# First pair's loads held until the last x tile has landed; the second FFN's rows normalised on ScalarE, its residual sum written in two halves

## The reference

```
x = x + 0.5 * ffn(layernorm(x))     # router to 8 experts, top 2, capacity 1537, softmax of the two logits
x = x + attention(layernorm(x))     # 16 heads of 16, rotary q and k, softmax, projection Wo and bias bo
x = x + 0.5 * ffn(layernorm(x))     # the same weights as the first
```

## Time and profile before

| what | value |
|---|---|
| median of three runs | 6290.88 us |
| the profiled execution | 6298.43 us, span 6296.6 us |
| TensorE busy | 6199.1 us (98%) |
| VectorE busy | 5929.1 us (94%) |
| ScalarE busy | 4830.8 us (77%) |
| POOL busy | 398.3 us (6%) |
| granted TensorE clock, mean | 0.988 |

### The profile page before, as it was taken

One profiled execution on the slowest core, in us unless ns is written; L12 is line 12 of the kernel. 1 busy time (PEld: TensorE's weight loads), 2 busy tenths in 40 slices (PEclk: granted clock), 3 DMA queues, 4 the chain that ended last, 5 costly groups with the idle time before them and its releaser, 6 DMA issues. The chain is left out here.

```text
span 6296.6 us, 158218 instructions
## 1 busy us (share of the span) xinstructions
PE 6199.1 (98%) x54276; PEld 2765.3 (44%) x54276; DVE 5929.1 (94%) x6835; ACT 4830.8 (77%) x8889; POOL 398.3 (6%) x604
## 2 busy tenths in 40 slices
PE   8998999999999999999999999999999999999999
PEld 6886333333333333333333333333333333334777
DVE  7998999999999999999999999999999999992877
ACT  4443488888888888888888888888888888886111
POOL 3443100000000000000000000000000000000221
PEclk9998699999999999999999999999999999999999
DMA  2334110101010101010101010101010101000110
GB/s 85 121 126 124 25 17 14 17 14 17 13 17 14 17 14 17 14 17 14 17 14 17 14 17 14 17 14 17 14 17 14 17 14 17 3 22 26 60 52 28
DMA packets 121411, 175.90 MB, mean 28 GB/s; under 512 B 62016, under 2 KB 78944, under 8 KB 117728
## 3 DMA queue, kind: packets, MB, share of 16 engines
q1 hardware_dynamic: 120928, 168.25, 11.8%
HBM read 98.47 MB, written 69.73 MB: 27 GB/s over the span
## 5 line engine op out<-in xcount | busy, mean ns | idle before, releaser
L1136 DVE TENSOR_REDUCE at_mx<-at_m 128x1 f32<-128x1024 f32 x4027 | 4927.9, 1224 | 47.6 <-PE at_m L1012 28.1
L1111 ACT ACTIVATE at_ex<-at_s 128x512 f32<-128x512 f32 x8192 | 4450.2, 595 | 612.9 <-PE at_s L1033 44.7
L1033 PE MATMUL at_s<-at_q,at_k 50*128 50x512 f32 x8192 | 2998.4, 444 | 0.0
L1012 PE MATMUL at_m<-at_k,at_q 48*128 48x512 f32 x8032 | 2927.1, 444 | 0.0
L1043 PE MATMUL at_po<-at_ex,at_v 128*32 128x256 f32 x32816 | 2625.8, 392 | 0.0
L1012 PEld LDWEIGHTS at_m<-at_k,at_q 48*128 48x128 f32 x8032 | 1184.3, 185 | 1658.7 <-DVE at_mx L1136 1590.5
L1043 PEld LDWEIGHTS at_po<-at_ex,at_v 128*32 128x32 f32 x32816 | 646.6, 108 | 1489.4 <-issue 749.9
L1033 PEld LDWEIGHTS at_s<-at_q,at_k 50*128 50x128 f32 x8192 | 1212.4, 185 | 42.6 <-ACT at_ex L1111 42.2
L987 POOL COPY at_v<-at_vst 128x1024 f32<-128x1024 f32 x16 | 16.7, 1041 | 4463.6 <-DMA at_vst<-v_by_head 4463.4
L1417 PE MATMUL bk_ps<-sh_weh,bk_xl 128*128 128x512 f32 x512 | 170.1, 413 | 20.2 <-DVE bk_acc L1547 20.1
L1459 ACT ACTIVATE bk_root<-bk_var 128x4 f32<-128x4 f32 x16 | 3.3, 205 | 218.0 <-DVE bk_var L1517 218.0
(11 more groups left out here) (194 smaller groups left out, 2989.9 us busy)
## 6 DMA issues: line engine op xcount, KB each, us to landing
at_q<-q_parts SPq DMA_DIRECT2D x96, 256.0 KB, 5.0
at_k<-k_parts SPq DMA_DIRECT2D x96, 256.0 KB, 6.3
q_parts<-fr_parts SPq DMA_DIRECT2D x64, 256.0 KB, 2.2
k_parts<-fr_parts SPq DMA_DIRECT2D x64, 256.0 KB, 2.4
attended<-at_o SPq DMA_DIRECT2D x256, 34.0 KB
fr_x<-in_x SPq DMA_DIRECT2D x16, 512.0 KB, 4.3
after_ffn<-fr_acc SPq DMA_DIRECT2D x16, 512.0 KB, 3.0
v_by_head<-fr_v SPq DMA_DIRECT2D x16, 512.0 KB, 4.4
```

The source lines that it names most:

```text
L1012: ins = pe.matmul(pm[w][:, h * QB:(h + 1) * QB], Q[p][rows, base + i * P:base + (i + 1) * P], K[p][rows, c * CW + h * QB:c * CW + (h + 1) ...
L1033: pe.matmul(ps[event(t) % NS], K[p][rows, j * P:(j + 1) * P], Q[p][rows, sb_ * QU + g * QB:sb_ * QU + (g + 1) * QB], start=True, stop=True ...
L1111: ac.activation(Ex[QUAD * (j % NX) + 2 * g + 1 - half][:, :], ps[event(t) % NS], ACT.Exp)\
L1136: ve.tensor_reduce(out=mx[u][:, i, c:c + 1], in_=first[(RED + k) % len(first)][:, 0:CW] if opens else pm[w][:, :], op=ALU.max, axis=AX.X)\
```

## The change

SP's wait: before the first pair's loads, SP waits until all x tiles of odd groups, the last of them tile 15, have landed. In the back phase, VectorE's `normal` becomes `newton`: the same five steps, and a sixth that forms nb = -mean * rs. ScalarE gets `normalise(g+1)`, four activations xn = src * rs + nb with per-row scale and bias, between the root and `turned`. The residual sum is cut in two calls: half 0 (tiles 0 and 1, from py[0]) follows the picks, half 1 stays at the body's end. Each half signals s_y, so all counts on s_y double, `spread_out` waits for half 0 of the previous group alone, and `project` gets a wait for both halves.

```diff
                     if isinstance(g, int) and g == NG - 2:
                         hold(sp, opening.s_one, 2, s_tick)
+                        hold(sp, s_x[(NG - 1) % 2], NG // 2 * DMA, s_tick)
                         for w in range(2):
...
                     pe.wait_ge(s_rec[u], it * DMA + DMA)
-                    need(pe, s_y, n)
+                    need(pe, s_y, n * 2 - 1)
                     pe.matmul(py[0][:, :], spread[:, :], rec[u][:, :], start=True, stop=True).then_inc(s_pr, 1)
...
                 def project(n):
                     need(pe, s_an, n + 1)
+                    need(pe, s_y, n * 2)
...
+                def normalise(n, src):
+
+                    need(ac, s_nw, (n + 1) * NEWTON)
+                    need(ac, s_tr, n)
+                    for i in range(TG):
+                        last = ac.activation(xn[:, i, :], src[:, i, :], ACT.Identity, bias=nb[:, i:i + 1], scale=rs[:, i:i + 1])
+                    last.then_inc(s_xn, 1)
...
                     if runs(g, 1):
                         take_root(g + 1)
+                        normalise(g + 1, y[1 - u])
                         turned(g + 1, 1 - u)
                         exponential(g + 1)
...
-                def add_residual(n, u):
-                    ve.wait_ge(s_py, n + 1)
-                    ve.wait_ge(s_xb, n + 1)
-                    for k in range(2):
-                        last = ve.tensor_tensor(y[u][:, 2 * k:2 * k + 2, :].rearrange("p i d -> p (i d)"), py[k][:, :],
-                                                xb[:, 2 * k:2 * k + 2, :].rearrange("p i d -> p (i d)"), ALU.add)
-                    last.then_inc(s_y, 1)
+                def add_residual(n, u, k):
+                    if k == 0:
+                        ve.wait_ge(s_py, n + 1)
+                        ve.wait_ge(s_xb, n + 1)
+                    ve.tensor_tensor(y[u][:, 2 * k:2 * k + 2, :].rearrange("p i d -> p (i d)"), py[k][:, :],
+                                     xb[:, 2 * k:2 * k + 2, :].rearrange("p i d -> p (i d)"), ALU.add).then_inc(s_y, 1)
...
-                def normal(n, src):
+                def newton(n):
 
                     ve.wait_ge(s_root, n + 1)
-                    ch = Chain(ve, s_nw, 5, n)
+                    need(ve, s_xn, n)
+                    ch = Chain(ve, s_nw, NEWTON, n)
...
+                    ch.add(ve.scalar_tensor_tensor(out=nb[:, :], in0=mv[:, :, 0], scalar=-1.0, in1=rs[:, :],
+                                                   op0=ALU.mult, op1=ALU.mult))
                     ch.close()
-                    need(ve, s_tr, n)
-                    for i in range(TG):
-                        last = ve.tensor_scalar(xn[:, i, :], src[:, i, :], mv[:, i, 0:1], rs[:, i:i + 1],
-                                                ALU.subtract, ALU.mult)
-                    last.then_inc(s_xn, 1)
...
                     if runs(g, 1):
                         pick(g + 1)
+                    if runs(g, 2):
+                        add_residual(g + 2, u, 0)
                     if isinstance(g, int) and g == 0:
                         invert_sums(ve, ahead, 1)
                     combine(g, u, it, 2, E // 2, E)
...
                     if runs(g, 2):
-                        add_residual(g + 2, u)
+                        add_residual(g + 2, u, 1)
```

More of the change, by code:

```diff
@@ L1258, in back_phase @@
     ROUTE = 7
+    NEWTON = 6
     with ExitStack() as ctx:
@@ L1278, in back_phase @@
         stats, mv = sb("stats", [P, TG, 6]), sb("mv", [P, TG, 2])
-        var, root, r0, r1, rs = (sb(n, [P, TG]) for n in ("var", "root", "r0", "r1", "rs"))
+        var, root, r0, r1, rs, nb = (sb(n, [P, TG]) for n in ("var", "root", "r0", "r1", "rs", "nb"))
         acc, acb = [sb(f"acc{u}", [P, TG, D]) for u in range(2)], sb("acb", [P, 2, D])
@@ L1476, in _ @@
                 take_root(0)
+                normalise(0, y[0])
                 turned(0, 0)
@@ L1496, in normalise_heads @@
                     last.then_inc(s_an, 1)
-                def add_residual(n, u):
-                    ve.wait_ge(s_py, n + 1)
-                    ve.wait_ge(s_xb, n + 1)
-                    for k in range(2):
-                        last = ve.tensor_tensor(y[u][:, 2 * k:2 * k + 2, :].rearrange("p i d -> p (i d)"), py[k][:, :],
-                                                xb[:, 2 * k:2 * k + 2, :].rearrange("p i d -> p (i d)"), ALU.add)
-                    last.then_inc(s_y, 1)
+                def add_residual(n, u, k):
[4 more added lines that the diff above has]
+                                     xb[:, 2 * k:2 * k + 2, :].rearrange("p i d -> p (i d)"), ALU.add).then_inc(s_y, 1)
                 def statistics(n, src):
-                    hold(ve, s_y, n + 1, s_tick)
+                    hold(ve, s_y, n * 2 + 2, s_tick)
                     for i in range(TG):
@@ L1592, in _ @@
                 normalise_heads(0, 0, 0)
-                add_residual(0, 0)
+                for k in range(2):
+                    add_residual(0, 0, k)
                 statistics(0, y[0])
-                normal(0, y[0])
+                newton(0)
                 normalise_heads(1, 1, 0)
@@ L1599, in _ @@
                 room(0)
-                add_residual(1, 1)
+                for k in range(2):
+                    add_residual(1, 1, k)
                 def body(g, u, it):
@@ L1607, in body @@
                     if runs(g, 1):
-                        normal(g + 1, y[1 - u])
+                        newton(g + 1)
                     combine(g, u, it, 1, 0, E // 2)
@@ L1634, in biased @@
                     if not (isinstance(n, int) and n == 0):
-                        hold(gp, s_y, n, s_tick)
+                        hold(gp, s_y, n * 2, s_tick)
                     for i in range(TG):
```

## The result

The changed kernel takes 6268.8 us (median of six runs, 6264.2 to 6273.7) beside 6291.6 of the kernel before (six runs, 6289.6 to 6301.9): 22.8 us less, a ratio of 0.9962 with a 95% interval of 0.9952 to 0.9972. Forecast were 6261.6 us, 29.3 less. Its profiled execution took 6268.08 us, span 6266.2, against 6298.43 and 6296.6 before; 30.4 us between the spans is more than between the medians, and the last experiments show which part of it is not the change.

The account below looks back on a forecast made before the run. TensorE, busy 98% of the span, was taken as the bound, so only its idle time could be won. Front 10.7 plus back 18.6 us gave 29.3 less, 6261.6 us; range 6251 to 6277 (own range 6256 to 6267).

Parts of the forecast that it names:

- the stall's size: Front, VectorE after its four statistics: the 12.22 us stall shrinks to 2.73, winning 9.4 us (bounds zero and 12.1).
- the clock: Front, TensorE after its gap: the clock stays at 2.4 GHz once the long gap goes, winning 1.3 us.
- group 0: Back phase, first group: of waits of 0.76 and 0.50 us, 0.5 is won; the inversion stays.
- 0.1 us for each turn: Back phase, TensorE's transposes: ScalarE's rows come level with need; 0.1 us a group charged, 15 x 0.1 = 1.5 us.
- The cover on SP: Front's end: later loads, issued near 518 and landed near 538, cost zero, hidden by 12 us on SP.
- The rule of the Trainium skill: Front: DMA engines serve rings in turn, so a backlog elsewhere holds no lone block; the front's gain would be zero.
- A group's 1.42 us: Back phase, TensorE's wait before the second tile's fourth chunk: 1.42 us won in each of twelve groups, 17.0 in all.
- Groups 13 and 14: Back phase, late groups: TensorE's waits give 2.0 us and 1.6 us; in the first of them the fetch stays.
- (a): Back phase: the turn takes over part of the wait; back 12.5, total 23.2 us, 6267.7; chance 0.14.
- (b): The front gives nothing: no fetch behind loads, or loads still catch a block; total 18.6 us, 6272.3; chance 0.18.
- (c): Back phase: ScalarE needs a 1.28 us table load before each group's rows; total 8.6 us, 6282; chance 0.04.
- (d): Start of attention: TensorE's clock stays half for longer; at 75 us more, 6299, slower than before; chance 0.04.

Follow-up runs that it names:

- the last experiments: The kernel before and the changed kernel each run once more, unchanged, for second traces: 6291.5 us and 6266.3 us.
- run 11: The kernel before once more, unchanged, for a second trace: 6291.5 us.
- run 12: The changed kernel once more, unchanged, for a second trace: 6266.3 us.
- run 4: The kernel before with only the residual sum cut in two halves, VectorE still normalising the rows: 6288.7 us, ratio 0.9992.
- run 7: The changed kernel with the second inversion of the sums in body 1 of the back phase instead of body 0: 6262.9 us.
- run 9: The changed kernel with the second inversion of the sums in the back phase's prologue instead of body 0: 6260.5 us, ratio 0.9948 to the kernel before.
- run 1: The kernel before with only SP's wait for the last x tile ahead of the first loads of attention: 6284.1 us, ratio 0.9983.
- run 10: The changed kernel with three small memsets on VectorE in the back phase's prologue: 6264.8 us.
- run 3: The kernel before with only the rows normalised on ScalarE, the residual sum left in one piece: 6278.6 us, ratio 0.9979.

## Why the prediction was right, and where it was off

The sign, the mechanism of both parts and the range were right; the gain was 6.5 us smaller than forecast. Two terms were too large (the stall's size and the clock), and one had the wrong sign (group 0). The two second traces, which have the same length of attention, differ by 23.4 us in span and show the steps:

```
step                                       predicted   measured (run 11 to run 12)
front, up to attention's first score         -10.7       -6.4   (707.5 to 701.0)
attention                                      0         +0.1
back, last score to first turn                +1.0       +0.8
turn 0 to 1                                   -0.4       -1.4
turn 1 to 2                                   -1.3       +3.4   (31.66 to 35.08)
turn 2 to 13, eleven periods                 -14.5      -16.1
turn 13 to 14                                 -1.9       -1.9
turn 14 to 15                                 -1.5       -1.6
behind turn 15                                 0         -0.3
```

(The forecast's 0.1 us for each turn is taken off in its rows.) That the back comes so close, 17.0 us for 18.6, is partly luck: turn 1 to 2 took 4.7 us more than forecast and the other rows together 3.2 less.

**The stall's size.** I took 12.22 - 2.73 = 9.4 us. Five traces without the held start show 12.22, 10.80, 9.61, 10.60 and 11.93, mean 11.0; six with the change's wait 2.99, 2.76, 3.63, 2.78, 3.74 and 3.45, mean 3.2. The step is right, its size is 7.8: the profiled 12.22 was the longest of five. The run with the front alone agrees, with 8.0 us. The 2.73 us that I took for an undisturbed stall come from a row that names TensorE as the releaser. It is a fetch stall all the same: in run 4 the same instruction idles 2.82 us down to "issue".

**The clock's 1.3 us** did not come. "That 1.3 us goes with the long gap" took the clock's fall as a matter of a long rest; some three us of rest are followed by a fall in the changed kernel's traces and in those of runs 7 and 9, and by none in runs 1 and 10. From VectorE's resuming to attention's first score it is 185.6 us in the mean of the five traces with the long stall, 185.7 in that of the four with a held start and a fall of the clock, and 183.2 in that of the two with a held start and no fall: where the clock fell nothing was won, where it held some 2.4 us, on two traces and with a spread of 2.4 within the five. (The first score itself comes at 701.4 us in the mean of the six and 708.2 in that of the five, only 6.7 apart, because the six happen to reach the stall 1.8 us later.)

**The cover on SP** held, though the loads were issued by 521.7 us and landed by 545.3, not by 518 and 538: SP's next work comes at 535.75, 14 us behind its last issue, and no reader waits.

**The rule of the Trainium skill** that spoke against the front's part ("DMA: Bandwidth & Descriptors", queues, rings and completion order: rings with work are served in turn, so a lone block isn't held by a backlog elsewhere) would have left the stall as it was. The measurement decides against that use of it: 11.0 us with the loads in flight, 3.2 without. A second rule of the Trainium skill, in "Runtime: NRT & Kernel Launch", instruction fetch mechanics, has blocks fetched ahead in order and mostly hidden. The "mostly" holds: in 5912 us of work the trace of the changed kernel puts only two idle times of VectorE over 0.3 us down to issue,

```profile
DVE bk_acb L1557 <- issue: 3.8, 1, 3.8
DVE fr_mv L566 <- issue: 3.0, 1, 3.0
DVE fr_acb L598 <- issue: 2.2, 12, 0.2
```

(time, count, longest). But those two stand in straight code, eight records behind a loop's exit and 87 behind the back's first residual sum, and the first of them reached TensorE (2.73 us); the second costs nothing by itself, by run 7.

**A group's 1.42 us** was 1.47, and without the 0.1 that I charged for the turn: ScalarE's four took 2.08 us, as the front's row said. Rows on ScalarE gave 1.19 and the halves 0.29, by the two runs that part them; 0.3 was my estimate of the second. Groups 13 and 14 came within 0.2 of theirs.

**Group 0 is the step that failed.** I wrote that the half sum is "hidden" behind the picks, and that in group 0 "the inversion stays". Turn 1 to 2 holds the end of body 0 and body 1's own wait; with that wait gone it should have been 30.2 us, and it is 34.7 to 35.1. In body 0 the half sum is ahead of the inversion, not just of combines, so it takes 0.6 us, and up to 1.13 of waiting for the projection (run 4), before the inversion can start; and the fetch stall, which in the kernel before falls on a combine that waits for TensorE anyway, now comes six records later, where VectorE has work, and idles it 3.78 us (see run 10). How late the inversion starts goes with what it costs:

```
                           reciprocal starts behind   period above the
                           its turn, us               kernel's usual one, us
before, second trace            8.2                        0.9
halves alone                    9.7                        2.4
inversion in body 1             9.7                        3.7
rows on ScalarE alone          11.4                        5.3
changed, first and second      11.4, 11.8                  5.4, 5.8
three instructions in prologue  10.5                        4.5
inversion in the prologue        -                         0.0
```

The shorter period has its part in it: at the same 9.7 us the inversion costs 2.4 where the usual period is 30.5 and 3.7 where it is 29.3. No run has the stall in group 0 ahead of the inversion at the old period, so how the two share the 5.4 to 5.8 is not parted further.

With the inversion out of group 0, more than all the gain that I had summed for the back is there: in run 9's trace the back is 22.8 us shorter than in the second trace of before, for a forecast of 18.6. Run 9 is 5.8 us under the changed kernel and so 31.1 under before. That this lies near the forecast's 29.3 is luck, of a front that gave less and a back that gave more.

**Rivals.** (a) is out: no wait at the turn. (b) is out: 8.0 us from the front alone. (c) is out: no table load. (d) is real as a thing that happens, up to 9.3 us in one execution, but it happened in the kernel before, and with the long gap and without.

Open: why the count of records begins anew in the back phase (87 with the eight instructions in the front and without), and why the clock fell behind some short rests. The traces show when a block moves and not where in memory it begins, nor whose it is, so the place of the boundary was inferred from the counts and not seen.

## What to carry to other kernels

When an engine stands still with no releaser in straight code, suspect the supply of its instructions, but look first whether another engine's instruction ended 0.1 us before it resumed, and whether a block moved on the instruction queue: "issue" alone is no proof, as the prologue's wait shows. Then put a few idle instructions ahead and see whether the stall moves; if it does, it can be moved to where the engine has slack, and large loads should not be issued just ahead of it. When the steady period of a loop gets shorter, look again at everything that happens once in it (a setup step, an inversion, a fetch): it was paid from slack that is gone, and it belongs in the prologue's idle time. And before a difference between two traces is told as the change's, take a second trace of one kernel: here 9 of 30 us were not.

## What the hardware showed that I had not expected

- An instruction block for VectorE took 2.60 to 4.35 us of stall (runs 9 and 3) where no large loads had been issued just ahead of it, and 9.6 to 12.2 behind loads of 3.6 MB issued 1 to 2 us before.
- Eight instructions ahead of the loop moved the front's stall by exactly 128 records of VectorE, with blocks of 8 KB on queue 14.
- TensorE's clock fell to half around a rest of 2.7 to 3.3 us in some executions, and not around rests of 2.7 and 3.5 us in others (0.50 for 518 to 520 us in the changed kernel, 1.00 with the front's part alone).
- The stretch at half clock at the start of attention cost the kernel before 9.3 us more in one execution than in another; the stretch ended near 731 us in one and near 709 in the other.
